# M's last heads loaded and split ahead of batch 0's context; the next q loaded on ScalarE's queue

## The chip, the cores and the metric

The kernel runs on one core of a Trainium2 chip. The metric is the device time of one execution in microseconds (us), as the median of several runs. A profile of one further execution gives the trace, whose times count from the first instruction of the span.

## The reference

A cross-attention block over 16 batches of 100 queries of width 640 (8 heads of 80). The context has 722 rows of width 384; its last 4 rows are split off as `ca`. All of it is in fp32.

```python
enc = encoder_hidden_states[:, :end_pos, :]      # 718 keys
ca = encoder_hidden_states[:, end_pos:, :]       # 4 tokens
query = hidden_states @ Wq
keyt = enc @ Wk
valt = enc @ Wv
hs = _mha(query, keyt, valt)
ca_q1 = jnp.einsum('btc,th->bch', ca, Wq_ca)[:, indices, :]
ca_hs1 = _mha(ca_q1, residual, residual)         # residual = hidden_states
ca_q2 = ca_hs1 @ Wq
ca_k2 = ca @ Wk_ca
ca_v2 = ca @ Wv_ca
ca_hs2 = _mha(ca_q2, ca_k2, ca_v2)
out = (hs + ca_hs2) @ Wout + b_out + residual
```

## The kernel before

Every fp32 product is computed from a high part and a low part of each factor: ScalarE copies the fp32 data into a tile of the matmul's type (the high part, semaphores that end in `hi`), and VectorE or GpSimd subtracts the high part from the data (the low part, semaphores that end in `lo`). TensorE multiplies high by high, high by low and low by high. Each operand therefore passes through load (SyncE, whose queue issues nearly all DMAs), high part (ScalarE), low part (VectorE or GpSimd) and matmul.

The order of work is written out by hand, once for each engine, and the engines meet only at semaphores. So an engine that waits in one place holds back everything written behind it on that engine.

**The first stage** (about the first 85 us) computes what all batches need. `query(g, j)` is one 128-row block (j) of q for a group (g) of four batches: 15 matmuls of 400 columns each, and for j = 5 the ten matmuls of `query_g` (L896, L901). `m_parts(n0, n1)` computes M, the product of Wq transposed with the keys of the 4 tokens: for each head h, five blocks c of three matmuls of 64 columns (L997), 40 parts in all. Each head's rows of Wq transposed are loaded by `load_heads` into the tile `probs` (L399), get their high part in `head_high` (L1255) and their low part in `head_low` (L1673); both parts go to `kstack` or `P1T`. TensorE waits for `hlo` before each head. The heads are loaded in three DMAs: heads 0 to 2, 3 to 5, and 6 and 7. Queries of group 1 and parts of M alternate on TensorE: `query(1, 4)`, then parts 28 to 33, in which head 6 begins at part 30, then `query(1, 5)` and parts 34 to 39, with head 7 from part 35. Behind them stand `query(2, 0)` and `keys(0, 0)`, the first block of batch 0's keys.

Batch 0's transposed context (718 keys, three blocks of 128 rows) is loaded in one DMA (L453), and split in `enc0_high` (L1265, three instructions) and `enc0_low` (L1645, three). `keys(0, 0)` waits for `enc0lo` and for two `m_low` (L1678), whose data are what `m_parts` has summed. The key blocks go to `kT` in `k_high` (L1154) and `k_low` (L1546), and from there by the DMAs of `lift` (L379, L382) to `kstack`, from which `scores` (L719) reads them. The staging of M uses the same storage, so `k_high(0, 0)` waits for `mst0`, the landing of the first two stores of M (L421).

**The batches** are a block of 420 matmuls each, in a loop over batches 1 to 14, with batches 0 and 15 written out. Per batch there are eight `scores` (L719), each with a maximum on VectorE (L1522), an exponential on ScalarE (`expo`, L1130), a normalisation (L1529), six transposes (`turn`, L760), and the high and low part of the result (L1141, L1535). Between them stand five blocks of the next batch's keys (L744) and six of the context (L779, L784). `qstack` holds q of one batch, in four DMAs of `load_q` (L333, L335), and is read by `scores`, so the next batch's q can be loaded only when `scores(i, 7)` is done. In the loop, `load_q(i + 1)` stands on SyncE's queue between `lift(i + 1, 0)` and `lift(i + 1, 1)`; in batch 0 it stands ahead of `lift(1, 0)`.

A tail multiplies the result by Wout and adds bias and residual.

Of the kernel before, what the change touches and what calls it, by code (L numbers as in the profile page):

```python
# [12 lines left out]
B, S, H = 16, 100, 640  # L13
HEADS = 8
# [49 lines left out]
def raw(ap):  # L64

    return ap.bitcast(F32)
# [25 lines left out]
def program(nc, x, xT, encT, encN, caT, asel, Wq, WqT, Wk, Wv, WqcaBD, Wkca, Wvca, Wout, bout, out,  # L92
            q_d, g_d, v2_d, m_d, hs_d):

    with ExitStack() as ctx:
# [223 lines left out]
        def halves(ap):  # L319
            return ap.rearrange("p (a k) -> p a k", a=2)  # L320

        with nc.Block() as block:
            @block.sync
            def _(sp):
                def free(name, n, first):
                    if not first:
                        wait_apart(sp, s[name], n, s["passed_sp"])

                def load_q(b, first=False):
                    free("scores", HEADS * b, first)  # L330
                    for p in range(2):
                        q3 = q_d[p].rearrange("(h d) n -> d h n", d=D)[:, :, bass.ds(b * S, S)]
                        sp.dma_start(raw(qst[p][0:D, :, :]), raw(q3)).then_inc(s["qin"], 16)  # L333
                        qh = q_d[0].rearrange("(h d) n -> d h n", d=D)[p * EX:(p + 1) * EX, :, bass.ds(b * S, S)]
                        sp.dma_start(raw(qst[p][D:STK, :, :]), raw(qh)).then_inc(s["qin"], 16)  # L335

                def load_encT(b, c, first=False):
                    free("encT", PARTS * (b - 2) + c + 1, first)
# [110 lines left out]
                load_x(0, first=True)  # L449
                sp.wait_ge(s["qst0"], 16 * 6)  # L450
                load_ga(0, first=True)
                sp.wait_ge(s["wlo"], 5)
                sp.dma_start(enc0_raw, encT[0].rearrange("(c p) k -> p c k", p=128)).then_inc(s["encin"], 16)  # L453
                sp.wait_ge(s["hlo"], 6)
                load_heads(6, 2)
                sp.wait_ge(s["v2st"], 32)
                load_q(0, first=True)
                store_q(1, 0, 3)
                store_q(1, 3, FT)
                store_g(1)  # L460
# [23 lines left out]
                def batch(i, first=False, last=False):  # L484
                    if last:
                        load_enc(i, 0)
                    else:
                        load_encT(i + 1, 0, first)
                    lift(i, 2, heads=(4,))
                    if last:  # L490
                        load_enc(i, 1)
                    else:
                        load_encT(i + 1, 1, first)
                    if not first:
                        store_hs(i - 1, 0)
                    lift(i, 3)
                    if last:
                        load_enc(i, 2)
                        sp.wait_ge(s["encT"], PARTS * (B - 1))
                        load_wo(0)  # L500
                    else:
                        load_encT(i + 1, 2, first)
                        if first:
                            wait_apart(sp, s["xTlo2"], 3 * FT, s["passed_sp"])
                        load_enc(i, 0, first)
                    lift(i, 4)
                    if last:
                        sp.wait_ge(s["wolo"], 2)
                        load_wo(1)
                    else:  # L510
                        load_enc(i, 1, first)
                        load_enc(i, 2, first)
                        load_ga(i + 1)
                        load_x(i + 1)
                    if first:
                        sp.wait_ge(s["encT"], PARTS)
                        sp.dma_start(wv_raw, tiled(Wv)).then_inc(s["wvin"], 16)
                        load_q(i + 1)
                    else:
                        wait_apart(sp, s["hsp"], 2 * i, s["passed_sp"])  # L520
                        load_v2(i)
                        if not last:
                            store_hs(i - 1, 1)
                    if not last:
                        lift(i + 1, 0)
                        if not first:
                            load_q(i + 1)
                        lift(i + 1, 1)
                        if first:
                            sp.wait_ge(s["q"], NP * GROUPS)  # L530
                            load_v2(i)
                        load_m(i + 1)
                        lift(i + 1, 2, heads=(3,))
# [589 lines left out]
            def _(act):  # L1123
# [169 lines left out]
                def batch(i, first=False, last=False):  # L1293
# [72 lines left out]
                    else:  # L1366
                        enc_high(i, 2)
                        k_high(i + 1, 0)
                    pt_high(i, 4, first)
                    expo(i, 7)  # L1370
                    if not last:
                        u_high(i, 0)
# [72 lines left out]
                xT_high(2, 3)  # L1445
                xT_high(2, 4)
                q_high(1, 2)
                for c in range(CT):
                    enc0_high(c)
                head_high(6)  # L1450
                q_high(1, 3)
                head_high(7)
                q_high(1, 4)
                q_high(1, FT)
                for c in range(FT):
                    m_high(c)
# [62 lines left out]
            def _(dve):  # L1519
# [283 lines left out]
                q_low(1, 1)  # L1803
                head_low(5)
                q_low(1, 2)
                for c in range(CT):
                    enc0_low(c)
                head_low(6)
                q_low(1, 3)
                head_low(7)  # L1810
                q_low(1, 4)
                q_low(1, FT)
                for c in range(FT):
                    m_low(c)
# [93 lines left out]
```

## Time and profile before

| | before |
|---|---|
| median of 3 runs | 1001.76 us (997.12 to 1004.11) |
| the profiled execution | 1004.24 us, of which its span 1002.5 us |
| busy, TensorE matmuls | 985.5 us (98%) |
| busy, VectorE | 652.0 us (65%) |
| busy, ScalarE | 490.8 us (49%) |
| busy, GpSimd | 342.9 us (34%) |
| mean busy share of the DMA engines, SyncE's queue | 75.6% |

Names of engines in the rows: PE is TensorE's matmuls, PEld its weight loads, DVE VectorE, ACT ScalarE, POOL GpSimd, SPq and ACTq the DMA issues of SyncE and ScalarE. L12 is line 12 of the kernel before. "x3" counts instructions that are merged in a row. A bracket tells how long the engine sat idle ahead of a row, and what ended that.

### The profile page before, as it was taken

What the parts mean: (1) busy time and instruction counts of PE and PEld (TensorE: products, weight loads), DVE (VectorE), ACT (ScalarE), POOL (GpSimd) and SP (SyncE); (2) the same over time, 40 slices, a digit from 0 to 9 for tenths busy, and PEclk for the clock granted to TensorE, in tenths of its full rate; (3) what the DMA queues carried; (4) which work ended last, traced back from release to release, by engine and by line L of the source; (5) the groups of instructions that cost most, each with busy time, mean ns of one, the idle gap of its engine ahead of it and who ended that gap; (6) DMA issues with size and microseconds to landing.
All of it is one profiled execution on the core that took longest, in us unless ns stands there. A gap on an engine that the chain in (4) does not pass through costs nothing.

```text
span 1002.5 us, 20727 instructions
## 1 busy us (share of the span) xinstructions
PE 985.5 (98%) x6740; PEld 964.2 (96%) x6740; DVE 652.0 (65%) x1129; ACT 490.8 (49%) x895; POOL 342.9 (34%) x286
## 2 busy tenths in 40 slices
PE   9989999999999999999999999999999999998998
PEld 8989889999999999999999999999999999997997
DVE  6544676667667766667676767676766666667444
ACT  7524555555554546464636364636464545446110
POOL 5212253434252516161515243333333333416000
PEclk9979999999999999999999999999999999999999
DMA  7959978797879797979797979788887878795354
GB/s 264 307 192 257 266 190 210 166 202 168 191 172 195 171 187 177 187 181 185 181 182 185 181 184 181 191 171 202 170 201 162 210 162 193 171 213 152 98 181 146
DMA packets 154169, 190.12 MB, mean 190 GB/s; under 512 B 80928, under 2 KB 108192, under 8 KB 154144
## 3 DMA queue, kind: packets, MB, share of 16 engines
q1 hardware_dynamic: 147456, 177.44, 75.6%
q10 hardware_dynamic: 6688, 12.35, 3.7%
q8 instruction: 15, 0.25, 0.1%
q14 instruction: 10, 0.08, 0.0%
HBM read 81.56 MB, written 19.95 MB: 101 GB/s over the span
## 4 chain that ended last, share of the span: by engine, by line
PE 85%; DVE 5%; SPq 4%; DMA 3%; ACT 2%; issue 1%; ACTq 0%; DVEq 0%
PE psS L744 21%; PE psB L779 20%; PE psB L784 10%; PE psS L719 7%; PE psT L760 6%; PE psS L888 6%; PE psT L806 4%; PE psT L812 2%; SPq L382 2%; DMA encT_raw<-in_encT_dram 1%; PE psB L861 1%; SPq L379 1%; PE psB L838 1%; PE psT L813 1%; PE psS L944 1%
## 5 line engine op out<-in xcount | busy, mean ns | idle before, releaser
L744 PE MATMUL psS<-encT_keep,Wk_keep 128*128 128x360 f32 x1440 | 253.7, 329 | 0.0
L744 PEld LDWEIGHTS psS<-encT_keep,Wk_keep 128*128 128x128 f32 x1440 | 237.3, 188 | 0.9 <-issue 0.2
L779 PE MATMUL psB<-PT_h,encN_h 120*128 120x400 f32 x576 | 202.3, 351 | 0.0
L779 PE MATMUL psB<-PT_l,encN_h 120*128 120x400 f32 x576 | 198.8, 345 | 0.0
L1130 ACT ACTIVATE probs<-psS,negmax 100x718 f32<-100x718 f32 x128 | 110.2, 861 | 129.2 <-DVE negmax L1522 129.0
L606 POOL TENSOR_TENSOR encT_keep<-encT_raw,encT_keep 128x718 fp32r<-128x718 f32 x45 | 79.7, 1771 | 181.6 <-ACT encT_keep L1159 179.3
L1546 DVE TENSOR_TENSOR kT<-psS,kT 128x718 fp32r<-128x718 f32 x80 | 72.4, 905 | 94.9 <-ACT kT L1154 94.7
L614 POOL TENSOR_TENSOR encN_l<-enc_raw,encN_h 120x768 fp32r<-120x768 f32 x48 | 92.6, 1930 | 91.4 <-ACT encN_h L1166 90.0
L597 POOL TENSOR_TENSOR Mbd<-Mbd,fmask 128x320 fp32r<-128x320 f32 x48 | 45.8, 954 | 226.7 <-DMA Mbd<-m_split 224.1
L784 PE MATMUL psB<-PT_h,encN_l 120*128 120x400 f32 x576 | 120.4, 344 | 0.7 <-POOL encN_l L614 0.7
L1154 ACT ACTIVATE kT<-psS 128x718 fp32r<-128x718 f32 x80 | 61.7, 771 | 115.2 <-PE psS L744 110.0
L1522 DVE TENSOR_REDUCE negmax<-psS 100x1 f32<-100x720 f32 x128 | 114.7, 896 | 0.0
L779 PEld LDWEIGHTS psB<-PT_l,encN_h 120*128 120x128 f32 x576 | 108.6, 189 | 0.0
L779 PEld LDWEIGHTS psB<-PT_h,encN_h 120*128 120x128 f32 x576 | 108.3, 188 | 0.2
L1535 DVE TENSOR_TENSOR PT_l<-psT,PT_h 120x600 fp32r<-120x600 f32 x128 | 99.5, 778 | 13.0 <-ACT PT_h L1141 8.8
L1551 DVE TENSOR_TENSOR UT<-psB,UT 128x400 fp32r<-128x400 f32 x96 | 54.9, 572 | 80.0 <-ACT UT L1172 80.0
L784 PEld LDWEIGHTS psB<-PT_h,encN_l 120*128 120x128 f32 x576 | 105.2, 188 | 1.2 <-POOL encN_l L614 1.1
L1172 ACT ACTIVATE UT<-psB 128x400 fp32r<-128x400 f32 x96 | 48.4, 504 | 115.1 <-PE psB L784 115.0
L719 PE MATMUL psS<-kstack,qstack_h 120*100 120x360 f32 x256 | 87.6, 342 | 1.0 <-DMA kstack<-kT 0.9
L760 PE MATMUL psT<-ident,probs 100*120 100x100 f32 x768 | 87.1, 249 | 1.0 <-DVE P L1595 0.6
L1141 ACT ACTIVATE PT_h<-psT 120x600 fp32r<-120x600 f32 x128 | 85.6, 669 | 4.1 <-PE psT L760 1.3
L1529 DVE TENSOR_SCALAR probs<-probs,inv 100x718 f32<-100x718 f32 x128 | 82.9, 648 | 4.5
(245 smaller groups left out, 1643.5 us busy)
## 6 DMA issues: line engine op xcount, KB each, us to landing
kstack<-kT SPq DMA_DIRECT2D x64, 448.8 KB
kstack<-kT SPq DMA_DIRECT2D x192, 112.2 KB
enc_raw<-in_encN_dram SPq DMA_DIRECT2D x48, 360.0 KB, 5.6
encT_raw<-in_encT_dram SPq DMA_DIRECT2D x45, 359.0 KB, 6.4
kstack<-kT SPq DMA_DIRECT2D x32, 359.0 KB
kstack<-kT SPq DMA_DIRECT2D x32, 269.2 KB
kstack<-kT SPq DMA_DIRECT2D x32, 179.5 KB, 3.6
kstack<-kT SPq DMA_DIRECT2D x64, 89.8 KB, 3.5
```

The costliest lines, as they stand in the source:

```text
L606: nc.gpsimd.tensor_tensor(eT[1][:, c, :], rawT[:, c, :], eT[0][:, c, :], ALU.subtract).then_inc(s["encT"], 1)
L614: nc.gpsimd.tensor_tensor(eN[1][:, ks, :], rawN[:, ks, :], eN[0][:, ks, :], ALU.subtract).then_inc(s["encN"], 1)
L719: mm = pe.matmul(psS[score_slot[h]][0:S, half, 0:HALF], qst[p][:, h, :], kst[:, p, h % SLOTS, k0:k0 + HALF], start=(p == 0), stop=(p == 1))
L744: mm = pe.matmul(keys_in(f, first)[:, half, 0:HALF], w[:, c, f * 128:(f + 1) * 128], e[:, c, k0:k0 + HALF], start=(j == 0), stop=(j == 3 * ...
L760: mm = pe.transpose(psT[0:KP, k // 3, (k % 3) * S:(k % 3 + 1) * S], P[h % PRING][0:S, k * KP:(k + 1) * KP], ident[0:S, 0:S])
L779: pe.matmul(psB[:, 1, 0:RH], eN[0][:, k, cc], PT[p][:, k, rows], start=(k == 0 and p == 0), stop=False)
L784: mm = pe.matmul(psB[:, 1, 0:RH], eN[1][:, k, cc], PT[0][:, k, rows], start=False, stop=(k == KT - 1))
L1130: nc.scalar.activation(halves(P[h % PRING][0:S, 0:KEYS]), without_overlap(psS[score_slot[h]], S), ACT.Exp, bias=negmax[:, h:h + 1], accum_ ...
L1141: nc.scalar.activation(PT[0][:, :, h * S:(h + 1) * S].rearrange("p (a k) n -> p a k n", a=2), psT[0:KP, :, 0:3 * S].rearrange("p a (k n) - ...
L1522: nc.vector.tensor_reduce(negmax[:, h:h + 1], tile_in(h), AX.XY, ALU.max, negate=True).then_inc(s["negmax"], 1)
L1529: nc.vector.tensor_scalar(P[h % PRING][0:S, 0:KEYS], P[h % PRING][0:S, 0:KEYS], inv[:, h:h + 1], None, ALU.mult).then_inc(s["norm"], 1)
L1535: nc.vector.tensor_tensor(o[1], psT[0:KP, :, 0:3 * S].rearrange("p a (k n) -> p a k n", k=3), o[0], ALU.subtract).then_inc(s["ptlo"], 1)
```

## The change

Two things are moved. In the first stage the load of heads 6 and 7 is issued ahead of the load of batch 0's context, and on ScalarE and VectorE the splits of the context move behind those of head 6, q(1, 3), head 7 and q(1, 4). In the batches, `load_q(i + 1)` moves from SyncE's queue to ScalarE's, between `pt_high(i, 4)` and `expo(i, 7)`, for batch 0 too. No arithmetic is added or removed.

```diff
+        def load_q(eng, b):
+            for p in range(2):
+                q3 = q_d[p].rearrange("(h d) n -> d h n", d=D)[:, :, bass.ds(b * S, S)]
+                eng.dma_start(raw(qst[p][0:D, :, :]), raw(q3)).then_inc(s["qin"], 16)
+                qh = q_d[0].rearrange("(h d) n -> d h n", d=D)[p * EX:(p + 1) * EX, :, bass.ds(b * S, S)]
+                eng.dma_start(raw(qst[p][D:STK, :, :]), raw(qh)).then_inc(s["qin"], 16)
...
@@ SyncE, first stage
                 load_ga(0, first=True)
+                sp.wait_ge(s["hlo"], 6)
+                load_heads(6, 2)
                 sp.wait_ge(s["wlo"], 5)
                 sp.dma_start(enc0_raw, encT[0].rearrange("(c p) k -> p c k", p=128)).then_inc(s["encin"], 16)
-                sp.wait_ge(s["hlo"], 6)
-                load_heads(6, 2)
                 sp.wait_ge(s["v2st"], 32)
-                load_q(0, first=True)
+                load_q(sp, 0)
@@ SyncE, a batch
                         sp.dma_start(wv_raw, tiled(Wv)).then_inc(s["wvin"], 16)
-                        load_q(i + 1)
...
                         lift(i + 1, 0)
-                        if not first:
-                            load_q(i + 1)
                         lift(i + 1, 1)
@@ ScalarE, a batch
                     pt_high(i, 4, first)
+                    if not last:
+                        act.wait_ge(s["scores"], HEADS * (i + 1))
+                        load_q(act, i + 1)
                     expo(i, 7)
@@ ScalarE, first stage (the same on VectorE with the low parts)
                 q_high(1, 2)
-                for c in range(CT):
-                    enc0_high(c)
                 head_high(6)
                 q_high(1, 3)
                 head_high(7)
                 q_high(1, 4)
+                for c in range(CT):
+                    enc0_high(c)
                 q_high(1, FT)
```

VectorE's order in the first stage, from the low part of head 5 on, before (`probs` is the loaded Wq transposed, `kstack` its split parts, `PT_l` the low part of q, `encT_keep` the split context):

```order
L1673 TENSOR_TENSOR kstack<-probs,kstack 80x640
L1667 SCALAR_TENSOR_TENSOR PT_l<-psB,PT_h 128x400
L1645 TENSOR_TENSOR encT_keep<-encT_raw,encT_keep 128x718 x3
L1673 TENSOR_TENSOR kstack<-probs,kstack 80x640
L1667 SCALAR_TENSOR_TENSOR PT_l<-psT,PT_h 128x400
L1673 TENSOR_TENSOR kstack<-probs,kstack 80x640
L1667 SCALAR_TENSOR_TENSOR PT_l<-psB,PT_h 128x400
L1667 SCALAR_TENSOR_TENSOR PT_l<-psB,PT_h 32x400
```

And the same place in the changed kernel, whose line numbers are one lower here:

```order
L1672 TENSOR_TENSOR kstack<-probs,kstack 80x640
L1666 SCALAR_TENSOR_TENSOR PT_l<-psB,PT_h 128x400
L1672 TENSOR_TENSOR kstack<-probs,kstack 80x640
L1666 SCALAR_TENSOR_TENSOR PT_l<-psT,PT_h 128x400
L1672 TENSOR_TENSOR kstack<-probs,kstack 80x640
L1666 SCALAR_TENSOR_TENSOR PT_l<-psB,PT_h 128x400
L1644 TENSOR_TENSOR encT_keep<-encT_raw,encT_keep 128x718 x3
L1666 SCALAR_TENSOR_TENSOR PT_l<-psB,PT_h 32x400
```

The three context splits have moved behind the low parts of heads 6 and 7 and of q(1, 3) and q(1, 4), and now stand directly ahead of the last, 32-row low part of group 1.

ScalarE's order in the loop, from the high part of the next batch's first key block to the high part of head 5's transposed probabilities, before:

```order
L1154 ACTIVATE kT<-psS 128x718
L1141 ACTIVATE PT_h<-psT 120x6x100
L1125 REGISTER_ALU
L1130 ACTIVATE probs,total<-psS,negmax 100x718
L1169 ISA
L1172 ACTIVATE UT<-psB 128x4x100
L1141 ACTIVATE PT_h<-psT 120x6x100
```

And in the changed kernel (its first line is L1150 where the one before has L1154):

```order
L1150 ACTIVATE kT<-psS 128x718
L1137 ACTIVATE PT_h<-psT 120x6x100
L1367 REGISTER_ALU
L325 ISA
L325 DMA qstack_h<-q_split 80x8x100
L327 DMA qstack_h<-q_split 40x8x100
L325 ISA
L325 DMA qstack_l<-q_split 80x8x100
L327 ISA
L327 DMA qstack_l<-q_split 40x8x100
L1121 REGISTER_ALU
L1126 ACTIVATE probs,total<-psS,negmax 100x718
```

Four DMA issues, with the wait for `scores` and the address work for them, now stand ahead of the exponential of head 7. SyncE's queue loses the same four; nothing else of its order in the loop moves.

## Rows read from the trace of the kernel before

**Rows 1.** Page, part 1, TensorE: busy us, share of the span, instructions
```profile
PE 985.5 (98%) x6740; PEld 964.2 (96%) x6740; DVE 652.0 (65%) x1129; ACT 490.8 (49%) x895; POOL 342.9 (34%) x286
```
**Rows 2.** Waits, TensorE, the longest group: waiter, releaser, us in total, times, longest
```profile
PE psS L997 <- DVE kstack L1673: 3.3, 2, 3.1
```
**Rows 3.** Windows: stretch, us, busy PE, PEld, DVE, ACT, POOL, granted clock, DMA share, GB/s
```profile
46.00:52.00 6.00, 5.87 (x43) 5.76 (x42) 4.14 (x3) 4.33 (x7) 5.69 (x5) 1.00 1.22 265
51.87:54.98 3.11, 0.00 (x1) 0.00 (x1) 3.11 (x3) 0.00 (x0) 2.84 (x3) 1.00 0.55 192
54.98:69.08 14.10, 14.10 (x54) 12.80 (x55) 5.35 (x9) 3.05 (x6) 0.46 (x2) 0.52 0.36 130
225.00:900.00 675.00, 674.56 (x4739) 664.56 (x4738) 462.55 (x831) 352.09 (x647) 246.40 (x193) 1.00 0.83 183
```
**Rows 4.** Timeline, 40 to 55 us: start, us, engine, line, operation, idle before
```profile
40.40 0.39 SPq L453 DMA_DIRECT2D encT_raw<-in_encT_dram  x1
43.57 0.33 SPq L399 DMA_DIRECT2D probs<-in_WqT_dram  x1
...
47.86 5.00 DVE L1645 TENSOR_TENSOR encT_keep<-encT_raw,encT_keep 128x718 fp32r<-128x718 f32 x3 [3.69 <-ACT encT_keep L1265]
...
52.79 2.13 DVE L1673 TENSOR_TENSOR kstack<-probs,kstack 80x640 fp32r<-80x640 f32 x1
...
54.98 2.63 PE L997 MATMUL psS<-kstack 80*128 80x64 f32 x12 [3.11 <-DVE kstack L1673]
```
**Rows 5.** Windows again: three stretches behind the stall, and the same work elsewhere
```profile
57.35:60.46 3.11, 3.11 (x11) 1.85 (x11) 0.00 (x0) 0.00 (x0) 0.00 (x0) 0.50 0.72 263
60.46:64.42 3.96, 3.96 (x20) 3.95 (x19) 0.56 (x1) 0.50 (x1) 0.00 (x0) 0.50 0.19 43
64.42:69.08 4.66, 4.66 (x16) 4.62 (x16) 3.08 (x5) 2.56 (x5) 0.00 (x0) 0.53 0.46 181
92.11:93.86 1.75, 1.75 (x11) 1.21 (x11) 1.16 (x3) 0.51 (x1) 1.42 (x2) 1.00 0.94 261
41.16:43.17 2.01, 2.01 (x18) 2.01 (x19) 2.01 (x4) 2.01 (x6) 0.00 (x0) 1.00 0.98 267
83.48:86.19 2.71, 2.71 (x16) 2.71 (x16) 0.91 (x1) 0.77 (x1) 0.55 (x1) 1.00 1.02 299
```
**Rows 6.** Line L1673, low parts of heads: duration ns min/median/max, first and last start
```profile
L1673 DVE TENSOR_TENSOR kstack<-probs,kstack x6: 807/813/2135, 25.8 to 55.3; 80x640 fp32r<-80x640 f32 x6
```
**Rows 7.** DMA issues: count, KB each, median us from issue to landing
```profile
encT_raw<-in_encT_dram SPq DMA_DIRECT2D x1, 1077.0 KB, 6.6
...
probs<-in_WqT_dram SPq DMA_DIRECT2D x1, 400.0 KB, 4.9
```
**Rows 8.** Timeline, 66 to 92 us: M's stores, first key block's high part, second scores
```profile
66.14 0.94 SPq L421 DMA_DIRECT2D m_split<-kT  x2
...
72.44 0.77 ACT L1154 ACTIVATE kT<-psS 128x718 fp32r<-128x718 f32 x1 [2.48 <-PE psS L744]
...
91.56 0.38 PE L719 MATMUL psS<-kstack,qstack_h 120*100 120x360 f32 x1 [0.89 <-DMA kstack<-kT]
```
**Rows 9.** Timeline, a batch of the loop, 496 to 504 us
```profile
496.38 0.33 PE L719 MATMUL psS<-kstack,qstack_l 120*100 120x360 f32 x1
...
498.35 0.86 ACT L1130 ACTIVATE probs<-psS,negmax 100x718 f32<-100x718 f32 x1 [2.18 <-DVE negmax L1522]
...
500.03 0.51 ACT L1172 ACTIVATE UT<-psB 128x400 fp32r<-128x400 f32 x1 [0.73 <-PE psB L784]
...
502.83 0.77 DVE L1535 TENSOR_TENSOR PT_l<-psT,PT_h 120x600 fp32r<-120x600 f32 x1
...
503.86 0.68 PE L760 MATMUL psT<-ident,probs 100*120 100x100 f32 x6
```
**Rows 10.** DMA issues on both queues by line: duration ns min/median/max, first and last start
```profile
L333 SPq DMA_DIRECT2D qstack_h<-q_split x16: 342/358/1103, 43.9 to 866.5; - x16
...
L1291 ACTq DMA_DIRECT2D q_split<-PT_l x5: 473/746/1037, 106.9 to 121.9; - x5
```

More of the change, by code:

```diff
@@ L327, in free @@
                         wait_apart(sp, s[name], n, s["passed_sp"])
[L329 to L335, printed above, removed]
                 def load_encT(b, c, first=False):
@@ L1805, in _ @@
                 q_low(1, 2)
-                for c in range(CT):
-                    enc0_low(c)
                 head_low(6)
@@ L1811, in _ @@
                 q_low(1, 4)
+                for c in range(CT):
+                    enc0_low(c)
                 q_low(1, FT)
```

## Prediction

> **What bounds the kernel now.** I read the page first: TensorE is busy 985.5 us of a span of 1002.5 us [rows 1], so all its idle time together is 17 us, and taking waits away can bring no more than that, unless TensorE's work itself gets faster. The windows view then says where the idle time lies. From 225 to 900 us, which is most of the loop, TensorE is idle 0.44 us of 675 and its granted clock is 1.00 [rows 3]. Nothing that moves in the loop can gain anything there; it can only lose. So the gain, if any, is in the first stage. The waits view gives its longest entry there: M's parts (L997) waited for VectorE's low parts of Wq transposed (L1673) for 3.3 us in two waits, the longest 3.1 [rows 2].
>
> The timeline shows why. The context's load is issued at 40.40, heads 6 and 7 at 43.57. VectorE then splits the context in three instructions from 47.86 to 52.86, and only behind them, at 52.79 (the ends of rows overlap a little), starts head 6's low part, which ends at 54.92. TensorE stood still until 54.98, for 3.11 us [rows 4]. VectorE's context split is not wanted by then: its reader, the first block of keys, starts at 69.08, where the last window of the slow stretch ends.
>
> The second thing the reader is to see is the column of the granted clock. It is 1.00 from 46 to 52 us, 1.00 through the stall, and 0.52 from 54.98 to 69.08 [rows 3]: right behind the 3.11 us of standing still, TensorE ran at the lower of its two levels, 1.2 GHz, for 14.1 us. So the stall has cost more than its length.
>
> **Part 1, the order in the first stage.** Taken away is the stall: 3.11 us. What the lower clock costs I take from the same work at either level [rows 5]. The row of 57.35 to 60.46 is one `query_g` (ten matmuls) at 0.50: 3.11 us; another `query_g` at 1.00, 92.11 to 93.86, takes 1.75: minus 1.36. The 18 matmuls of M from 60.46 to 64.42 take 3.96; 18 of the same kind from 41.16 to 43.17 take 2.01: minus 1.95. `query(2, 0)`, 15 matmuls from 64.42 to 69.08, takes 4.66; another query block from 83.48 to 86.19 takes 2.71: minus 1.95. The twelve parts from the stall's end at 54.98 to 57.35 take 2.37; twelve eighteenths of 2.01 are 1.34: minus 1.03. Together 6.29 us, and with the stall 9.40 us. From the stall's start, 51.87, to the first block of keys the path was 17.21 us and would be 7.81.
>
> Is everything in time at this pace? *Head 6:* its 400 KB take 4.9 us [rows 7], so from the same issue at 43.57 they land at 48.5 at the latest; in front of them one load of 1077 KB less is in the queue. The high part I estimate at 0.75 us, a little under VectorE's fast 0.81 for the same size [rows 6]. The low part takes 0.81 us as a median and 2.13 at most [rows 6]; the slow one ran while GpSimd was busy 2.84 of 3.11 us, and from 46 to 52 us GpSimd is busy 5.69 of 6.00 [rows 3], so I take the slow one: 48.5 + 0.75 + 2.13 = 51.4, against 51.87. Tight, but in time. *Head 7:* behind q(1, 3)'s low part, some 0.6 us, it takes another 2.13 at most, 54.1, and is wanted one part behind `query_g`, at 51.87 + 1.34 + 1.75 + 0.33, or 55.3. *The context:* its load takes 6.6 us [rows 7] from about 43.95, so it has landed by 50.6, and its high parts are made behind q(1, 4), about 52 to 54. VectorE's three low parts took 5.00 us, 1.67 each [rows 4], with GpSimd busy; GpSimd is nearly idle behind 55 (0.46 of 14.10 us, [rows 3]). Starting at 54.7 they end at 59.7 at the latest. The first block of keys would start at 51.87 + 7.81 = 59.7. It also wants two low parts of M, which now stand behind the context's splits and one more low part: an estimate of 1.9 us for the three, from the 813 ns of 640 columns [rows 6] at 400 to 512, so 61.6 if VectorE keeps its slow pace; if the splits speed up without GpSimd as the heads' low parts do (0.81 us against 2.13), they and M's two end before 59. Between a wait of 0 and one of 1.9 us I take 0.2, since GpSimd's work there is over. *M's stores:* they were issued from 66.14, and the high part of the first key block at 72.44 waited for TensorE, not for them [rows 8]. They may now be issued up to 1 us later against M's end, while TensorE gets from M's end to the end of the first keys in 1.95 us less. Between 0 and 1 us, which would pass on through SyncE's lifts to the scores that at 91.56 already waited 0.89 us for a lift [rows 8], I take 0.2.
>
> **Part 2, q on ScalarE's queue.** It removes four issues per batch from SyncE and puts them, with a wait for `scores(i, 7)`, ahead of `expo(i, 7)`. SyncE's gain is worth nothing, as the loop's idle 0.44 us says. The price on ScalarE comes from one batch. The last matmul of scores 7 starts at 496.38 and ends at 496.71. ScalarE was idle 2.18 us until the exponential at 498.35, for VectorE's maximum [rows 9]. So the wait for the scores costs nothing, and 1.6 us of issuing lie under VectorE's maximum. Queued behind them are the exponential, the high part of the context product at 500.03, which itself followed 0.73 us of idle time, and through its low part and a chain of small operations on VectorE the low part of head 5 at 502.83, which ends at 503.60 ahead of its reader, the transposes at 503.86 [rows 9]. The cover is 1.6 + 0.73 + 0.26 = 2.6 us. Four issues cost 4 x 0.36 = 1.4 us by the row of these issues on SyncE's queue; by the low-part stores on ScalarE's queue, 0.75 us in the median, 3.0 us [rows 10]. The first is these very transfers, and an order of high then low would average less than the second, so I take 2.0 with the address work: hidden. Without the cover it would be 14 times the excess. Batch 0's copy I put at up to 0.5 us, taken as 0. The loads themselves, 750 KB per batch, now start some 6 us earlier and beside the lifts of the next batch's first key block. The Trainium skill (DMA: Bandwidth & Descriptors, Issuing engines are not separate DMA queues) says that issuing from several engines saves only the sequencer's time, since all transfers share the same DMA engines. By that rule, too, the second part gains nothing; it adds that the lifts and q would interleave, a loss if lifts have no slack. No row here shows the two side by side.
>
> **Sum.** 9.40 - 0.2 - 0.2 = 9.0 us against the profiled execution's 1004.24 us: 995.2. That execution lies 2.5 us above the median of the runs, 1001.76, and nothing in the change scales with that, so against the median it is 992.8 us, 0.9% less.
>
> **The rivals.**
> *A. Another stall takes its place.* The head loads land late, or the first keys wait 1.9 us for M's low parts, and the scores 1 us for their lift: 9.4 - 2.9 = 6.5, or 995.3. If TensorE stands still for some 3 us again, the lower clock comes back too, and of 9.4 us perhaps 3 are left: 998.8. For it: head 6 has a margin of 0.5 us. Against it: every bound above was the slow one. 14 in 100.
> *B. ScalarE's issues reach beyond their cover.* At 3.0 us per batch against 2.6, 14 x 0.4 = 5.6 us are lost: 1001.76 - 9.0 + 5.6 = 998.4. 12 in 100.
> *C. Slower.* The same mechanism, with issues as long as the longest of those rows, 1.04 us: 4.15 us per batch, 1.55 beyond the cover, 14 times 21.7 us: 1014.5. It turns the sign from 2.6 + 9.0 / 14 = 3.2 us per batch on. Against it: SyncE's own q issues have a median of 0.36 us. 5 in 100.
> *D. Nothing changes*, since head 6's load or its high part, not VectorE, was about to be late by as much, or since the clock falls in this stretch of narrow matmuls anyway. Against it: the same mixture of query blocks and parts of M ran at 1.00 from 46 to 52 us [rows 3]. 1001.8. 5 in 100. The Trainium skill (TensorE: Matmul & The Clock Gate, What's actually happening) describes the clock as throttled by default and released by activity; by that an idle stretch, not the kind of matmul, brings the fall, as the row of the stall and the one behind it agree.
> *E. More than 10 us.* The 0.89 us wait at 91.56 goes as well and no slip comes: 10.3, or 991.5. 6 in 100.
>
> **How the numbers follow.** The forecast, a gain of 8 to 10 us with the loop unchanged, has 58 in 100: 991.8 to 993.8, and 992.8 as its middle. The range takes in E, A's two cases and B: 990.5 to 999.0; C, D and the tails stay out. A measurement of this kernel can tell about 1%, 10 us, from no change, and the forecast lies 1 us inside that. Faster by over 1%: E and a third of the forecast, 0.26. Slower by over 1%: C, 0.04. Within: 0.70.
>
> **What would show it.** In the changed profile the granted clock of 50 to 70 us is 1.00, and M's parts wait under 0.5 us for L1672; the first keys start near 60 and the second scores near 82.5. VectorE's context splits take under 5 us, between 54 and 60. A batch of the loop takes the same time as before, TensorE's idle share there stays under 0.2%, and the exponential of head 7 starts at most 0.5 us later behind its scores. The prediction is wrong if the clock is low there without a stall, if a wait of over 1 us stands ahead of the first keys, or if the loop grows at all.

## The result and the profile after

| | before | changed |
|---|---|---|
| median | 999.57 us (997.12 to 1004.11, 4 runs) | 1012.88 us (1010.82 to 1017.55, 4 runs) |
| ratio to before | | 1.0134 [1.0079, 1.0189] |
| the profiled execution | 1004.24 us, span 1002.5 | 1012.8 us, span 1011.1 |
| busy, TensorE matmuls | 985.5 us | 986.5 us |
| DMA share of SyncE's queue (q1) and ScalarE's (q10) | 75.6% and 3.7% | 67.9% and 10.3% |

The change costs 1.3% where a gain of 0.9% was forecast (a second series of runs, below, gave a cost of 0.6%). Its first half did what it should, and its second half lost more than the first gained. In all rows below a line number of the changed kernel is a few lower than that of the same line before: L1154 is L1150 here, L719 is L715, L1673 is L1672.

The changed kernel's windows, with the columns of [rows 3]:

```profile
33.00:38.00 5.00, 5.00 (x17) 4.96 (x18) 0.00 (x0) 1.14 (x1) 0.00 (x0) 0.50 1.02 318
46.00:60.00 14.00, 14.00 (x101) 13.43 (x101) 6.57 (x8) 4.93 (x8) 7.77 (x8) 1.00 1.04 307
60.00:70.00 10.00, 10.00 (x59) 10.00 (x59) 5.07 (x11) 4.34 (x8) 0.00 (x0) 1.00 0.82 302
225.00:900.00 675.00, 664.96 (x4636) 649.03 (x4635) 441.32 (x813) 340.72 (x633) 243.87 (x192) 1.00 0.80 178
```

From 46 to 70 us TensorE is never idle and its clock is 1.00: the stall of 3.11 us and the slow stretch behind it [rows 3] are gone. But there is a slow stretch at 33 to 38 us. The profiled execution of before did not have it, as this window of it shows:

```profile
25.00:40.00 15.00, 14.90 (x104) 14.46 (x103) 6.22 (x9) 6.12 (x10) 0.20 (x1) 1.00 1.01 330
```

The last row of the changed kernel's windows is the loop: TensorE, idle for 0.44 us of these 675 before, is now idle for 10.04. Taken between the loads of `v2bd` in batches 1 and 14, thirteen batches take (863.87 - 173.65) / 13 = 53.09 us each, against (856.03 - 179.86) / 13 = 52.01 before. Of these 14.1 us more, 9.0 are idle time of TensorE; the other 5.0 stand in the profile as busy time of the same 4747 matmuls (680.83 us against 675.79), and what stretches it is not shown. The first of these loads is issued 6.2 us earlier than before, so the gain of the first stage is there, and 14 batches at 1.08 us give back 15.1.

The changed kernel's waits (waiter, releaser, us in total, times, longest), whole run and then TensorE alone from 165 to 900 us:

```profile
ACT kT L1150 <- DMA kstack<-kT: 56.6, 14, 5.4
```
```profile
PE psB L822 <- DVE P L1562: 6.6, 11, 0.8
PE psS L715 <- DVE kT L1545: 3.6, 5, 1.1
```

`L1150 <- DMA kstack<-kT`, once per batch, is new: in this stretch of the kernel before, the view shows no wait of ScalarE for a lift at all. The high part of a key block goes into `kT`, from which the lifts of an earlier block must have been read. Its 56.6 us are of ScalarE, which has time to spare; the two groups of TensorE are what comes through. The chain of work that ended last, by line, agrees; the line of the lifts, `DMA kstack<-kT`, holds 9% of it:

```profile
PE psB L775 14%; PE psS L740 14%; DMA kstack<-kT 9%; PE psB L780 7%; PE psS L715 7%; PE psS L884 6%; SPq L381 4%; PE psT L756 4%; PE psT L802 4%; PE psT L808 2%; SPq L378 2%; PE psB L919 2%; DVE PT_l L1534 1%; ACT kT L1150 1%; PE psS L993 1
```

One batch in order of time, the changed kernel's timeline (columns of [rows 4]):

```profile
495.75 0.72 SPq L378 DMA_DIRECT2D kstack<-kT  x1
495.83 0.32 ACTq L325 DMA_DIRECT2D qstack_h<-q_split  x1
496.25 0.41 ACTq L327 DMA_DIRECT2D qstack_h<-q_split  x1
496.51 2.39 SPq L381 DMA_DIRECT2D kstack<-kT  x2
496.82 0.38 ACTq L325 DMA_DIRECT2D qstack_l<-q_split  x1
497.36 1.52 ACTq L327 DMA_DIRECT2D qstack_l<-q_split  x1
498.80 0.68 PE L756 MATMUL psT<-ident,probs 100*120 100x100 f32 x6
499.05 0.86 ACT L1126 ACTIVATE probs<-psS,negmax 100x718 f32<-100x718 f32 x1 [3.92 <-issue]
499.81 1.46 SPq L381 DMA_DIRECT2D kstack<-kT  x2
502.83 0.68 PE L756 MATMUL psT<-ident,probs 100*120 100x100 f32 x6
507.97 0.77 ACT L1150 ACTIVATE kT<-psS 128x718 fp32r<-128x718 f32 x1 [3.47 <-DMA kstack<-kT]
```

The scores of head 7 end at 495.68. The four q issues on ScalarE (ACTq) run from 495.83 to 498.88, 3.05 us, beside the first lifts on SyncE. Still the transposes at 498.80 and 502.83 keep the distance of 4.03 us that they had before, when they stood at 499.83 and 503.86 [rows 9]. The time is lost behind them, at 507.97. The chain in this stretch (start, us, what) goes from the last group of SyncE's lifts of block 0 through a landing:

```profile
499.81 0.77 SPq L381
500.57 0.04 issue
500.62 7.27 DMA kstack<-kT
...
507.97 0.78 ACT kT L1150
508.77 0.62 DVE kT L1545
...
511.51 0.42 PE psB L822
511.93 0.77 PE psS L715 x4
```

So a lift issued by 500.6 held `k_high(i+1, 2)`, the third key block's high part, until 507.97. In the kernel before, the same instruction waited only for TensorE's sums:

```profile
507.81 0.77 ACT L1154 ACTIVATE kT<-psS 128x718 fp32r<-128x718 f32 x1 [2.28 <-PE psS L744]
```

Windows of the same five us of a batch, first of the changed kernel, then of the one before (1.03 us later, as its scores end at 496.71):

```profile
497.00:502.00 5.00, 5.00 (x33) 4.72 (x31) 1.78 (x6) 2.01 (x5) 4.33 (x4) 1.00 1.08 223
```
```profile
498.03:503.03 5.00, 5.00 (x32) 4.72 (x31) 2.67 (x6) 2.22 (x5) 4.34 (x4) 1.00 0.81 202
```

The DMA share there rises from 0.81 to 1.08 (a share can exceed 1.00 in this view): q's 750 KB, which used to start at 502.59, come in beside the lifts.

### The profile page after: what moved, and what is told of

Its sections match the earlier page's. It is cut to its first block, busy times and chain, and to the rows that moved or that the text cites. A ratio compares the mean times of both kernels' runs of the same rounds, so it can differ in the third digit from the quotient of the medians.

```text
span 1011.1 us, 20740 instructions
## 1 busy us (share of the span) xinstructions
PE 986.5 (98%) x6740; PEld 959.0 (95%) x6740; DVE 638.6 (63%) x1129; ACT 487.2 (48%) x895; POOL 341.0 (34%) x286
## 3 DMA queue, kind: packets, MB, share of 16 engines
q1 hardware_dynamic: 117876, 165.91, 67.9%
q10 hardware_dynamic: 36268, 23.88, 10.3%
## 4 chain that ended last, share of the span: by engine, by line
PE 68%; DMA 12%; SPq 7%; DVE 7%; ACT 3%; issue 1%; ACTq 1%; DVEq 0%
PE psB L775 14%; PE psS L740 14%; DMA kstack<-kT 9%; PE psB L780 7%; PE psS L715 7%; PE psS L884 6%; SPq L381 4%; PE psT L756 4%; PE psT L802 4%; PE psT L808 2%; SPq L378 2%; PE psB L919 2%; DVE PT_l L1534 1%; ACT kT L1150 1%; PE psS L993 1%
## 5 line engine op out<-in xcount | busy, mean ns | idle before, releaser
L1150 ACT ACTIVATE kT<-psS 128x718 fp32r<-128x718 f32 x80 | 61.7, 772 | 140.9 <-PE psS L740 78.0
L715 PE MATMUL psS<-kstack,qstack_h 120*100 120x360 f32 x256 | 89.1, 348 | 4.7 <-DVE kT L1545 4.5
```

Of the source, the lines that this page charges most:

```text
L715: mm = pe.matmul(psS[score_slot[h]][0:S, half, 0:HALF], qst[p][:, h, :], kst[:, p, h % SLOTS, k0:k0 + HALF], start=(p == 0), stop=(p == 1))
```

## The experiments

Three causes of the loss could be told apart: ScalarE held by the issues (rival B and C's mechanism), q's data beside the lifts, and the queue from which they come. Two questions stood on the first stage: what it is worth alone, and what of it is order and what is loads. Each kernel was timed beside the kernel before, in three groups on three chips, so ratios and periods are compared and not times. "Period" is the time per batch in the loop, taken as above from the profile; it was 52.01 us before.

### Each half alone

The first stage of the change, with `load_q` back on SyncE's queue where it was:

```diff
                         lift(i + 1, 0)
+                        if not first:
+                            free("scores", HEADS * (i + 1), False)
+                            load_q(sp, i + 1)
                         lift(i + 1, 1)
...
                     pt_high(i, 4, first)
-                    if not last:
-                        act.wait_ge(s["scores"], HEADS * (i + 1))
-                        load_q(act, i + 1)
```

> Only the first stage is changed (heads 6 and 7 loaded and split ahead of batch 0's context); q stays on SyncE's queue at its old place. Transfer theory (the q transfers, begun 6 us earlier and beside the lifts of the next key block, delay those lifts) and issue theory (the 3.0 us of issuing on ScalarE delay what is queued behind it) both expect the loss of the loop to be gone: a batch of the loop takes 52.1 us again, and the first stage gains 6 to 9.4 us, so 0.991 to 0.994 of the time before. Rival (the first stage's new timing disturbs the loop): 53 us per batch, 1.005 or more.

Measured: 997.89 us, ratio 0.9954 [0.9931, 0.9977], period 52.08.

And `load_q` on ScalarE's queue with the first stage of the kernel before (the edit is the change without its first-stage part):

> Only load_q moves to ScalarE's queue; the first stage is as before. Transfer and issue theory: 14 batches of 53.2 instead of 52.1 us, 15 us slower than before, 1.015, and the stall of 3.1 us with the low clock behind it is there as before. Rival (first stage to blame): 1.00.

Measured: 1015.90 us, ratio 1.0137 [1.0089, 1.0185], period 53.17, and the wait again:

```profile
ACT kT L1150 <- DMA kstack<-kT: 57.2, 14, 5.6
```

The two halves are separate. The first stage gains 0.5%. The move of q loses 1.4% on its own and 1.8% on top of the first stage (1.0% by the second series of the changed kernel below). In the profiles its loss lies in the loop.

### ScalarE held, with no transfer

To the first-stage kernel, at q's place between `pt_high(i, 4)` and `expo(i, 7)`, seven small copies into a spare tile are added, and q stays on SyncE:

```diff
                     pt_high(i, 4, first)
+                    if not last:
+                        act.wait_ge(s["scores"], HEADS * (i + 1))
+                        for n in range(7):
+                            nc.scalar.activation(
+                                pad[:, :].rearrange("p (o n) -> p o n", o=2),
+                                ident[0:S, 0:100].rearrange("p (o n) -> p o n", o=1).to_broadcast([S, 2, 100]),
+                                ACT.Copy).then_inc(s["padded"], 1)
+                            act.wait_ge(s["padded"], 7 * i + n + 1)
                     expo(i, 7)
```

> As e1, and ScalarE is held for about 3 us in each batch by seven small copies into a scratch tile, at the place where the changed kernel issues q, behind the same wait for the scores. No transfer moves. Issue theory: the exponential of head 7 starts some 1.7 us later and a batch takes 53.2 us, 15 us slower than e1. Transfer theory: as e1 within 3 us.

Measured: 997.89 us, ratio 0.9953 [0.9928, 0.9978], period 51.97. ScalarE's timeline shows the hold at the place of the issues:

```profile
489.25 2.79 ACT L1375 ACTIVATE pad<-ident 100x200 f32<-100x200 f32 x7 [0.58 <-PE psS L721]
492.20 0.86 ACT L1132 ACTIVATE probs<-psS,negmax 100x718 f32<-100x718 f32 x1 [0.17 <-ACT pad L1375]
```

From the start of the hold to the exponential it is 2.95 us, against 3.22 with the four issues (495.83 to 499.05), and nothing is lost. The hold is 0.27 us shorter than the issues, so ScalarE's time could explain at most 0.27 of the 1.08 us per batch. Rivals B and C fall as the mechanism of the loss: ScalarE had the time to give.

### The same early q, on SyncE's queue

`load_q(i + 1)` in front of `lift(i + 1, 0)` on SyncE, as soon as `scores(i, 7)` is done:

```diff
                     if not last:
+                        free("scores", HEADS * (i + 1), False)
+                        load_q(sp, i + 1)
                         lift(i + 1, 0)
```

> As the changed kernel, but q is issued on SyncE's queue, directly ahead of the lifts of the next batch's first key block; ScalarE issues nothing in the loop. Transfer theory (q's 750 KB, begun before those lifts are out, make them land late, and the third key block's high part, which needs the storage they read, waits): the loss stays, 52.8 us per batch or more, at least 10 us slower than e1. If only the second queue's interleaving or ScalarE's part in it counts: as e1, 52.0 us per batch.

Measured: 1003.38 us, ratio 1.0014 [0.9985, 1.0042], period 52.40. ScalarE waits for the same lifts, in the profile's waits:

```profile
ACT kT L1152 <- DMA kstack<-kT: 46.7, 14, 3.7
PE psB L824 <- DVE P L1561: 1.9, 7, 0.5
```

and in one batch, SyncE's and ScalarE's rows:

```profile
498.40 1.48 SPq L381 DMA_DIRECT2D kstack<-kT  x2
...
504.36 0.77 ACT L1152 ACTIVATE kT<-psS 128x718 fp32r<-128x718 f32 x1 [3.26 <-DMA kstack<-kT]
```

Against the first stage alone it loses 0.6%, 0.32 us per batch: by the period about a third of what the changed kernel loses, and less than the 52.8 us or more that was expected. The lifts here are issued later (the last of block 0 by 499.88, 7.6 us behind the scores' end at 492.28; in the changed kernel by 501.27, 5.6 us behind it) and yet ScalarE's wait is shorter, since `k_high` follows the last of them by 4.5 us and not by 6.7.

As the issues on SyncE leave ScalarE free, one more kernel combined this with the hold of seven copies:

> As e4 (q on SyncE's queue ahead of the lifts; 5.5 us slower than e1), and ScalarE is held for 2.8 us by small copies where the changed kernel issues q, as in e5 (which alone cost nothing). If the rest of the loss, from e4's 52.4 to the changed kernel's 53.1 us per batch, comes from the late exponential together with the late lifts, this kernel takes 53.1 and about 1013 us. If it comes from the transfers of two queues taking turns, it takes 52.4 and about 1003 us, as e4.

Measured: 1001.49 us, ratio 0.9996 [0.9972, 1.0020], period 52.26. The hold adds nothing to the early q either. So the other 0.7 us of the 1.08 per batch belong neither to ScalarE's time nor to a sum of the two: they appear only when q is issued from ScalarE's queue, beside the lifts. Whether the second queue as such does it, or that the first lifts are then issued among q's transfers and not behind them, no run here separates. By the times the share is also less clear than by the periods: against the second series of the changed kernel (1.0057), the early q on SyncE's queue (1.0014) has more than half of the loss.

### Half of q early

Of the four transfers the two of the high parts (375 KB) stay early on ScalarE, and the other two go back to SyncE's old place:

```diff
                         act.wait_ge(s["scores"], HEADS * (i + 1))
-                        load_q(act, i + 1)
+                        load_q(act, i + 1, (0,))
```

> As the changed kernel, but only the first half of q (two of the four DMAs, 375 KB) is issued early on ScalarE's queue; the other half is issued by SyncE at its old place. Transfer theory: the lifts are delayed by about 2 us instead of 4, less than half of the loss is left, and the wait of the third key block's high part for lifts shrinks from 4 us (idle ScalarE in all) to the 2.3 us it has behind TensorE; 52.4 us per batch or less. A theory of the count of queues alone: the full loss.

Measured: 997.44 us, ratio 0.9951 [0.9927, 0.9976], period 52.04, and no wait of L1155 for a lift among ScalarE's longest in the loop. Half the data on the second queue costs nothing: the loss has a threshold, as a wait behind slack has.

### q on ScalarE, one block later

`load_q` on ScalarE's queue behind `pt_high(i, 5)` instead of `pt_high(i, 4)`, some 4 us later behind the scores:

```diff
                     pt_high(i, 5)
+                    if not last:
+                        act.wait_ge(s["scores"], HEADS * (i + 1))
+                        load_q(act, i + 1)
```

> As the changed kernel, but the four q issues on ScalarE stand one step later, behind the high part of head 5's transposed probabilities, some 5 us later in a batch and about 1.5 us ahead of where SyncE issued them. Transfer theory: the lifts of the first key block are mostly out by then, and at most a third of the loss is left, 52.5 us per batch or less. Issue theory: ScalarE is held as long, ahead of the next keys' high part and the high part of P2, and the loss of about 1 us per batch stays or grows.

Measured: 1004.78 us, ratio 1.0032 [1.0004, 1.0060], period 52.45. In the loop none of ScalarE's longest waits is for a lift any more, yet something is lost, and TensorE's waits name another chain, the small products behind `P2x`. The control holds ScalarE for 2.8 us at this place, without a transfer:

> As e1, and ScalarE is held for 2.8 us behind the high part of head 5, where e3 issues q; no transfer moves. If e3's 7 us over e1 come from ScalarE being held ahead of the exponential of the small scores and the next keys' high part, this loses as much, 1003 to 1006 us. If they come from q's transfer, it is as e1, 998 us.

Measured: 1006.33 us, ratio 1.0048 [1.0017, 1.0080], period 52.59. TensorE's waits from 165 to 900 us, of q on ScalarE there, then of the hold:

```profile
PE psB L869 <- DVE P2x L1616: 1.9, 5, 0.6
```
```profile
PE psB L875 <- DVE P2x L1627: 5.4, 14, 0.4
```

The hold alone loses at least as much as q did. So here ScalarE's time is enough to explain the loss, and nothing is left for the transfer: the two places change roles. Behind head 4 ScalarE has slack and the lifts have too little; behind head 5 it is the other way round.

### The first stage, taken apart

The order of loads as before (context ahead of heads 6 and 7), with the splits in the new order:

```diff
-                sp.wait_ge(s["hlo"], 6)
-                load_heads(6, 2)
                 sp.wait_ge(s["wlo"], 5)
                 sp.dma_start(enc0_raw, encT[0].rearrange("(c p) k -> p c k", p=128)).then_inc(s["encin"], 16)
+                sp.wait_ge(s["hlo"], 6)
+                load_heads(6, 2)
```

> As e1, but SyncE loads the context ahead of heads 6 and 7 again, so only the splits are moved. If VectorE's splits were what made head 6 late, this is as e1 (0.995). If the load's place matters too, it is slower than e1 by 1 to 3 us.

Measured: 999.37 us, ratio 0.9975 [0.9948, 1.0002], period 52.02. And the kernel before with only the third of the three context splits moved behind head 6:

```diff
-                for c in range(CT):
+                for c in range(CT - 1):
                     enc0_low(c)
                 head_low(6)
+                enc0_low(CT - 1)
```

> The kernel before, with only the last of the three context splits moved behind head 6's; loads and q as before. Where the stall ahead of head 6 appears at all, it is 1.4 instead of 3.1 us. If the long stall is what lowers the clock in the slow executions of the kernel before, their clock is back: mean clock as e1's (0.996), median as e1's (997.9 us) within 1.5 us. If the clock falls for another reason, the mean clock stays at 0.994 and the median at 1001 or so.

Measured: 999.51 us, ratio 0.9980 [0.9952, 1.0009], period 51.98. Both lie between no change and the whole first stage (0.9954), and both intervals overlap it and 1.00, so these two don't split the gain. What they gave was their profiles, which are read below.

### The two kernels once more

> The changed kernel once more, for a second trace and beside the same runs of before: 1.013 of their time; 53.1 us per batch; the third key block's high part waits for lifts in all 14 batches of the loop. The stretch of low clock in the first stage need not lie where it lay the first time.

Measured: 1007.91 us (1003.86 to 1014.25, 10 runs), ratio 1.0057 [1.0031, 1.0083]; the profiled execution took 1014.25 us at a period of 53.12, with 54.0 us of ScalarE's wait for lifts. Slower again, but by less, and with a spread of 10 us, where the ratio of the first measurement was 1.0134. The two intervals overlap only between 1.0079 and 1.0083. The profiled execution, which was the slowest of these runs, has the full loss. Not all the others can have it: the fastest run of the first stage alone took 994.95 us, and with 15.1 us more that is 1010, but six of these ten runs took less.

> The kernel before once more, for a second trace of its first stage. If the 3.1 us stall and the 14 us at the low clock behind it belong to every execution, they are there again, and the mean clock is 0.992. If they belong to some executions only, the first stage shows a shorter stall or none, and a time of some 997 to 1001 us with a clock of 0.995 or more.

Measured: one execution, 1005.8 us, span 1004.1. It has the stall and the slow stretch again (TensorE's wait, then windows):

```profile
PE psS L997 <- DVE kstack L1673: 3.5, 2, 3.0
```
```profile
25.00:40.00 15.00, 14.44 (x101) 14.01 (x100) 5.99 (x9) 5.13 (x8) 0.59 (x1) 1.00 1.01 326
52.00:60.00 8.00, 4.96 (x24) 3.99 (x24) 5.23 (x5) 0.43 (x1) 3.72 (x4) 0.75 0.51 184
60.00:70.00 10.00, 10.00 (x39) 9.56 (x38) 3.65 (x6) 3.05 (x6) 0.00 (x0) 0.52 0.39 139
```

## Why the prediction was wrong

**The step that failed** is the end of part 2: "The loads themselves, 750 KB per batch, now start some 6 us earlier and beside the lifts of the next batch's first key block", for which the sum held nothing, and no rival stood for it. It was named and left without a price. They start 5.7 us earlier against the scores' end, the lifts land later, and ScalarE's third key block waits for them in every batch. The mean idle time ahead of that instruction is 4.0 us (56.6 / 14), against 2.28 in the batch of the kernel before, where TensorE ended it; 1.8 us late, of which some 0.7 are taken up behind it and 1.08 reach TensorE. In the early q on SyncE the idle time is 46.7 / 14 = 3.3 us, 1.0 us late, and 0.39 reach TensorE by its period: about the same 0.7 of slack, an estimate from the two pairs. Fourteen times 1.08 is the 15 us that turn a gain of some 4 us into a loss. The Trainium skill (DMA: Bandwidth & Descriptors, Issuing engines are not separate DMA queues) says that transfers of all engines share the same 16 DMA engines and interleave. The trace agrees as far as it can: with both queues at work the share of those engines is 1.08 against 0.81, and a lift issued 0.9 us behind q's last issue took 7.27 us to land. The prediction used this rule for "gains nothing", added "a loss if lifts have no slack", and then did not ask how much slack they have.

**The row that would have told.** The slack could have been estimated before: the high part at 507.81 followed 2.28 us of ScalarE's idle time, which TensorE ended (2.3 us in each of the 14 batches), and the lifts that it needs were issued by 502.41 on the timeline of before, so 5.4 us were there for them, and they were never late. Over the loop (225 to 900 us) the two kinds of lifts that the landing view times took 3.7 and 3.9 us in the median. A transfer put beside them had some 1.5 us to spend, an estimate. It is a rough one: these medians are over the lifts of all blocks, and in the changed kernel they are lower (3.3 and 3.6 us), although the lifts of block 0 are late there.

**The issues' time** was mis-sized too, without harm. Instead of 2.0 us they took 3.05, with 1.23 to 1.65 us for each batch's fourth, and 3.22 us from the first issue to the exponential, beyond the cover of 2.6 us. By the prediction's own working this would have cost 0.45 to 0.62 us in every batch. The hold, 2.95 us to the exponential, cost nothing, so the cover was larger than 2.6: the exponential at 499.05 started 1.7 us later behind its scores than before (3.37 us behind 495.68, against 1.64 behind 496.71), and the high part of the context product followed at 499.90 with no idle time, 0.9 us later behind the scores than before. Yet the low part of head 5 started at 501.79, 6.1 us behind the scores' end, just as before (502.83). One small subtraction of VectorE between them gave the 0.9 us back, first before, then in the changed kernel:

```profile
501.56 1.34 DVE L1606 TENSOR_TENSOR P<-P,st 100x32 f32<-100x32 f32 x1
501.42 0.44 DVE L1605 TENSOR_TENSOR P<-P,st 100x32 f32<-100x32 f32 x1
```

Both end 0.04 us behind the end of GpSimd's product that writes `gbd` (502.85 before, 501.82 changed). So it is in all 14 batches before, in 13 of 14 of the changed kernel (0.33 to 0.73 us), and in all of the held one (0.82 us); the one time that it started behind GpSimd's product it took 0.19 us. So some 1.1 of its 1.34 us were time in which it could start later at no cost, a part of the cover that the sum left out.

**Rival C** had the sign, and 1014.5 us was near the 1012.88 measured, but by another mechanism: it needed issues of 1.04 us each. It is no hit.

**Part 1 did what it said.** Its expected marks in the changed kernel's timeline, low parts of heads 6 and 7, the context's low parts, and the second scores:

```profile
49.23 1.31 DVE L1672 TENSOR_TENSOR kstack<-probs,kstack 80x640 fp32r<-80x640 f32 x1 [4.02 <-ACT kstack L1251]
50.95 1.17 DVE L1672 TENSOR_TENSOR kstack<-probs,kstack 80x640 fp32r<-80x640 f32 x1
55.51 2.54 DVE L1644 TENSOR_TENSOR encT_keep<-encT_raw,encT_keep 128x718 fp32r<-128x718 f32 x3
...
84.56 0.38 PE L715 MATMUL psS<-kstack,qstack_h 120*100 120x360 f32 x1 [0.24 <-DMA kstack<-kT]
```

Head 6 is there at 50.5, head 7 at 52.1, the context's three low parts take 2.54 us instead of 5.00, M's parts wait for none of them, and the clock from 46 to 70 us is 1.00. The two slips of 0.2 us each can't be told apart from the rest. (The "twelve parts" of the prediction from 54.98 to 57.35 are twelve matmuls, four parts; its sum is not touched by that.) The second scores come at 84.56, 7.0 us earlier than before and not at the 82.5 forecast. The slow stretch at 33 to 38 us, ahead of all this, can account for the 2.1 us between them: the next profile is late by as much behind the same stretch.

**But the 9.0 us were the price of one kind of execution.** The first stage alone gained 0.46%, 4.6 us. The same first stage has executions of two kinds. The kernel with q moved alone has the first stage of before, unchanged; its profile, though, has no stall. Its windows, and TensorE and VectorE around head 6:

```profile
33.00:38.00 5.00, 5.00 (x17) 4.96 (x17) 0.00 (x0) 1.48 (x1) 0.00 (x0) 0.50 1.03 312
```
```profile
51.91 1.67 DVE L1672 TENSOR_TENSOR kstack<-probs,kstack 80x640 fp32r<-80x640 f32 x1
...
53.99 0.42 PE L993 MATMUL psS<-kstack 80*128 80x64 f32 x3
```

There the clock is already low from 32 to 39 us. That makes TensorE late by 2.1 us at head 6 (it starts at 53.99, where it stood ready at 51.87 [rows 3]), VectorE is done by 53.58, and neither the stall nor the 14 us at half clock follow. The profile of the kernel with only the third split moved has the early slow stretch too, and no stall. The change can take 9 us only from executions of the first kind. One of its relatives shows the other end: the kernel with the loads in the old order has neither the early slow stretch nor a stall in its profile, and that execution took 995.46 us, beside the 995.2 that the sum gave against 1004.24; it was the fastest of that kernel's twelve (up to 1002.29). Over the runs made side by side with the first stage alone (29 of the kernel before, median 1001.97, and 12 of it) the mean granted clock goes from 0.9942 to 0.9964, worth 2.2 us, and the mean time less what the clock took (the time, times what the mean clock lacks to 1) from 996.2 to 994.6, 1.6 us; together 3.8, beside 4.1 between the medians.

**Another stall took part of the gain back**, at the other end of the kernel. In the profile of the first stage alone the load of `v2bd` in batch 1 comes 7.0 us earlier than before (172.90 against 179.86). But from that load in batch 14 to the one in batch 15 it takes 60.71 us (849.89 to 910.60) against 53.79 before, 6.9 us more. Between them TensorE and ScalarE wait:

```profile
PE psB L850 <- DVE P1T L1582: 5.4, 1, 5.4
ACT Wk_keep L1210 <- DMA encT_raw<-in_Wout_dram: 6.2, 1, 6.2
```

The load of Wout, issued in batch 15, landed 11.6 us behind its issue, against 7.4 before; ScalarE waited for it ahead of the high part that TensorE needed, TensorE stood still for 5.4 us (1.2 before), and the granted clock is 0.50 from 900 to 910 us (1.00 before). The same wait of TensorE is 3.0 us in the held kernel's profile, 3.5 in those of half of q and of the one split moved, and 4.1 in the second one of the changed kernel, but 1.6 in that of the loads in the old order and in the second one of the kernel before. The change does not touch this load. Why it lands late, and in how many executions, stays open; it is a stall as in rival A, in a place that the prediction did not look at.

The prediction took its whole gain from one execution and set against it the median of runs; it reckoned with 2.5 us between the two and did not ask whether those 2.5 were this very stall.

## What to carry to other kernels

Before a load is moved earlier, look at what moves data in its new place, and how long before their readers those transfers are issued; that lead less their landing time is the slack, and here it was some 1.5 us by an estimate. Moving issues to an engine with free time says nothing on whether the transfers have room: hold the engine without the transfer, and send the transfer from the old queue, and the two causes come apart. A stall seen in one profiled execution should be looked for in a second before its price is put into a sum.

## What was not expected of the hardware

- **A second queue hurt more than an earlier place on the same one.** The same 750 KB, started 5.7 us earlier from ScalarE's queue, cost 1.08 us per batch; from SyncE's queue ahead of the lifts, 0.25 to 0.4 us, at the same DMA share (1.08 against 1.07 over five us). The queues' totals show what was moved: q10 went from 6688 packets and 12.35 MB to 36268 packets and 23.88 MB, so q is 29580 packets of about 390 bytes. The third high part followed the last lift's issue by 6.7 us beside them, and by 4.5 us when q had gone first on its own queue. That the engines take turns between the two queues, so that lifts give way to q for as long as both have packets, would fit; no run shows the turns themselves, so this stays open.
- **The loss varies between executions**, from 1.0134 to 1.0057 in ratio, though ScalarE's wait was 56.6, 57.2 and 54.0 us in three profiles. What differs in the quicker executions was not profiled. The series that lost 0.6% and the one in which q moved alone lost 1.4% ran on different chips, and whether that matters is open.
- **The last issue of a series was long.** In the changed kernel the q issues on ScalarE took 0.32 to 0.42 us for the first three, and 1.23 to 1.65 for the fourth; on SyncE's queue, ahead of the lifts, 0.30 to 0.40 for all four. In a batch of the kernel with q behind head 5 the third was the longest, at 0.92 us.
- **The clock can fall without a long stall.** In the executions of the second kind it fell to 0.50 at about 32 us, with TensorE idle for only 0.57 us at 30.5 ahead of it; two other profiles (the kernel before once more, and the loads in the old order) have 0.56 us idle at the same place and a clock of 1.00 from 25 to 40 us. Four others lie between, with a clock of 0.89 over 25 to 40 us. The Trainium skill (TensorE: Matmul & The Clock Gate, What's actually happening) has the throttle released by activity, and the 3.0 and 3.1 us of idle time ahead of the slow stretch at 55 us and the 5.4 us ahead of 903 us agree with it. The fall at 32 us has no such idle time in front of it here, and its cause is open.
- **VectorE ran the same subtraction at different speeds.** The context's three low parts took 5.00 us beside a busy GpSimd and 2.54 beside an idle one; a head's 0.81 us to 2.13; and the small one above ended with GpSimd's product wherever it had started before that product's end.
